# A graph network's first layer on one core: half of the type one-hots moved from VectorE to ScalarE, multiplied one chunk later

## The reference, cut to what matters

```python
def rel_layer(h, src, dst, etype, norm, V, comp, loop_w, bias, activation):
    c = comp[etype]                       # (100000, 8): a row of 8 coefficients by the edge's type
    m = 0
    for b in range(8):
        m = m + c[:, b, None] * (h @ V[b])[src]
    agg = segment_sum(m * norm, dst)
    out = agg + bias + h @ loop_w
    return relu(out) if activation else out

h = relu(layernorm(x))
x = x + rel_layer2(rel_layer1(h))         # both with the same etype, norm, src and dst
h = relu(layernorm(x))
x = x + gcn(relu(gcn(h)))                 # deg, the degree of a node, scales its rows
```

## Time and profile before

| | us |
|---|---|
| median of 3 runs (lowest, highest) | 2038.98 (2038.0, 2039.23) |
| the profiled execution | 2035.34 |
| its span, from the first to the last instruction | 2033.6 |
| busy in the span: TensorE, VectorE | 1691.0, 1404.2 |
| busy in the span: GpSimd, ScalarE | 1403.0, 356.8 |

### The profile page before, as it was taken

One profiled execution on the slowest core, in us unless ns is written; L12 is line 12 of the kernel. 1 busy time (PEld: TensorE's weight loads), 2 busy tenths in 40 slices (PEclk: granted clock), 3 DMA queues, 4 the chain that ended last, 5 costly groups with the idle time before them and its releaser, 6 DMA issues. The chain is left out here.

```text
span 2033.6 us, 40639 instructions
## 1 busy us (share of the span) xinstructions
PE 1691.0 (83%) x12305; PEld 1214.2 (60%) x12306; DVE 1404.2 (69%) x2294; ACT 356.8 (18%) x869; POOL 1403.0 (69%) x1527
## 2 busy tenths in 40 slices
PE   1488888788788888888389988889999899968998
PEld 1366556566566565566366666666676666745564
DVE  7898888888888878886677566566666657511533
ACT  2032222222222222222101111011011101100300
POOL 5777777777777777777477777777777777777000
PEclk8589889889899899898699888899999899978999
DMA  5334343343343333332222222233232332334473
GB/s 149 92 101 113 94 109 98 96 109 97 92 112 94 93 110 94 98 102 71 72 61 62 60 60 59 58 84 100 85 102 68 82 97 77 92 94 127 148 238 118
DMA packets 194039, 196.66 MB, mean 97 GB/s; under 512 B 109132, under 2 KB 157273, under 8 KB 193946
## 3 DMA queue, kind: packets, MB, share of 16 engines
q0 software_dynamic: 45760, 93.81, 16.8%
q1 hardware_dynamic: 140134, 97.59, 16.5%
q10 hardware_dynamic: 8052, 4.04, 0.7%
HBM read 169.75 MB, written 25.57 MB: 96 GB/s over the span
## 5 line engine op out<-in xcount | busy, mean ns | idle before, releaser
L811 POOL DMA_INDIRECT ring<-h_rows,rel_idx x1312 | 1257.7, 959 | 400.5 <-issue 365.4
L986 DVE TENSOR_TENSOR rel_pick<-rel_src_row,dve_bank 128x1664 bf16<-128x1664 int32 (+1 forms) x268 | 486.0, 1814 | 176.9 <-PE rel_ps_p L1215 93.4
L1284 PE MATMUL rel_ps_z<-rel_C,ring 128*128 128x56 f32 x3100 | 417.9, 284 | 166.6 <-DMA ring<-h_rows,rel_idx 83.2
L1284 PEld LDWEIGHTS rel_ps_z<-rel_C,ring 128*128 128x128 f32 x3100 | 399.4, 200 | 219.0 <-issue 209.8
L1382 ACT ACTIVATE rel_ZT<-rel_ps_z 128x304 f32 x292 | 114.2, 426 | 1071.3 <-PE rel_ps_z L1284 1069.7
L1228 PE MATMUL rel_ps_p<-rel_h_parts,rel_pick 128*128 128x384 bf16 x1150 | 266.8, 363 | 0.0
L1372 ACT ACTIVATE rel_A<-rel_ps_a 128x500 f32 x292 | 165.6, 603 | 391.3 <-PE rel_ps_a L1172 206.2
L1215 PE MATMUL rel_ps_p<-rel_h_parts,rel_pick 128*128 128x384 bf16 x1100 | 202.2, 345 | 22.0 <-DVE rel_h_parts L974 22.0
L1215 PE MATMUL carried<-rel_h_parts,rel_pick 128*128 128x384 bf16 x1100 | 190.7, 332 | 2.4 <-DVE rel_pick L986 2.4
L1172 PE MATMUL rel_ps_a<-rel_M,rel_lo 128*128 128x175 bf16 x784 | 156.8, 296 | 38.3 <-DVE rel_M L953 38.1
L1215 PEld LDWEIGHTS rel_ps_p<-rel_h_parts,rel_pick 128*128 128x128 bf16 x1100 | 113.4, 105 | 100.2 <-issue 39.5
(11 more groups left out here) (232 smaller groups left out, 1699.6 us busy)
## 6 DMA issues: line engine op xcount, KB each, us to landing
ring<-h_rows,rel_idx POOLq DMA_INDIRECT x1312
A_slabs<-rel_A SPq DMA_DIRECT2D x25, 800.0 KB
A_slot<-A_slabs SPq DMA_DIRECT2D x25, 800.0 KB, 4.5
rel_types<-edge_types SPq DMA_DIRECT2D x97, 200.0 KB
early_slot<-A_slabs SPq DMA_DIRECT2D x18, 896.0 KB, 6.1
rel_src_row<-in_src_dram SPq DMA_DIRECT2D x134, 64.0 KB, 3.0
last_slot<-A_slabs SPq DMA_DIRECT2D x4, 512.0 KB, 6.0
ring<-h_rows,idx_table POOLq DMA_INDIRECT x118
```

Source lines behind the costliest of these rows:

```text
L811: g_.indirect_dma_start(ring[:, s * CHUNK + i, :], None, rows_in, bass.IndirectOffsetOnAxis(ap=idx[which][:, n:n + 1], axis=0)).then_inc(l ...
L986: v.tensor_tensor(pick[:, b0:b0 + n, :], src_row[s][:, :].unsqueeze(1).to_broadcast(shape), node_ids[:, b0:b0 + n].unsqueeze(2).to_broadca ...
L1284: ins = m_.matmul(bank(ps_z[s], NB)[:, :, bass.ds(at[i], TW)], ring[:, first + i, :], C[s][:, i, :, :], start=False, stop=(i == n - 1))
```

## The change

The one-hot of types 0 to 99 stays on VectorE. That of types 100 to 199 is made on ScalarE in two passes over the types t: first (t - k)^2, k being the partition's type number (as a bias of -k, `less_type`), then relu(1 - that), which is 1 where t = k and 0 elsewhere (bias 1, `one_col`). ScalarE makes it after its two copies of A and before its copy of ZT. The type product stands one chunk later on TensorE: in chunk c that of c + 5, not of c + 6, while the one-hots are still made for c + 6. The sums follow one chunk later too (`scale` of c + 4, not c + 5). The degree product moves on TensorE from behind the type product to ahead of the picks of its chunk. The waits of GpSimd for type products are lowered by one where the product moved. `prepare` gets one memset and one small VectorE operation for the two bias tables.

```diff
@@ prepare @@
+            g.memset(t.one_col[:, :], 1.0).then_inc(consts_set, 1)
...
+            v.tensor_scalar(t.less_type[:, :], t.type_id[0:RH, :], -1.0, None, ALU.mult)
@@ new class @@
+class SharedCoefficients(Coefficients):
...
+    def load(self, eng, m, s):
+        after(eng, self.upper_ready, m - 1)
+        super().load(eng, m, s)
+
+    def make_onehot(self, eng, m, quarter_m, s):
+
+        after(eng, self.product_done, m - 1)
+        eng.wait_ge(self.etype_in[s], (quarter_m + 1) * 16)
+        self.nc.vector.tensor_scalar(self.onehot[:, s % 2, 0, :], self.etype[:, s % 2, :], self.t.type_id[0:RH, 0:1],
+                                     None, ALU.is_equal).then_inc(self.onehot_ready, 1)
+
+    def make_upper(self, act, m, quarter_m, s):
+
+        after(act, self.product_done, m - 1)
+        act.wait_ge(self.etype_in[s], (quarter_m + 1) * 16)
+        upper = self.onehot[:, s % 2, 1, :]
+        self.nc.scalar.activation(upper, self.etype[:, s % 2, :], ACT.Square, bias=self.t.less_type[:, 1:2]).then_inc(self.squared, 1)
+        act.wait_ge(self.squared, m + 1)
+        self.nc.scalar.activation(upper, upper, ACT.Relu, bias=self.t.one_col[:, 0:1], scale=-1.0).then_inc(self.upper_ready, 1)
+
+    def multiply(self, eng, m, s):
+        eng.wait_ge(self.upper_ready, m + 1)
+        super().multiply(eng, m, s)
@@ GpSimd, half_way and ahead_of @@
-                    hold(pool, co.product_done, at + (AHEAD + 1) if not (isinstance(c, int) and at + (AHEAD + 1) > ET_CHUNKS) else ET_CHUNKS)
+                    hold(pool, co.product_done, at + AHEAD if not (isinstance(c, int) and at + AHEAD > ET_CHUNKS) else ET_CHUNKS)
...
-                    begun = {(5, 0): 1, (5, 1): 3, (6, 0): 5, (6, 1): 6, (7, 0): 7, (7, 1): 8}
+                    begun = {(5, 0): 1, (5, 1): 3, (6, 0): 4, (6, 1): 5, (7, 0): 6, (7, 1): 7}
@@ VectorE @@
                     co.make_onehot(dve, m, m // 4, m % 4)
-                    if m:
-                        co.scale(dve, m - 1, m - 1)
+                    if m >= 2:
+                        co.scale(dve, m - 2, m - 2)
...
-                    if layer == 0 and not (isinstance(c, int) and c + AHEAD - 1 >= ET_CHUNKS):
-                        co.scale(dve, c + (AHEAD - 1), (parity * CPG + j + AHEAD - 1) % COEF_RING)
+                    if layer == 0 and not (isinstance(c, int) and c + AHEAD - 2 >= ET_CHUNKS):
+                        co.scale(dve, c + (AHEAD - 2), (parity * CPG + j + AHEAD - 2) % COEF_RING)
@@ TensorE @@
-                for m in range(AHEAD):
+                for m in range(AHEAD - 1):
                     co.multiply(pe, m, m % 2)
...
                         sum_slab(c, j % 2, at)
+                    if layer == 0 and j == 3 and not is_first:
+                        degrees(g - 1)
...
-                    if makes(g, j):
-                        co.multiply(pe, c + AHEAD, j % 2)
+                    if layer == 0 and not (isinstance(c, int) and c + AHEAD - 1 >= ET_CHUNKS):
+                        co.multiply(pe, c + (AHEAD - 1), (j + 1) % 2)
...
-                    if layer == 0 and j == 3 and not is_first:
-                        degrees(g - 1)
@@ ScalarE @@
+            for m in range(AHEAD if layer == 0 else 0):
+                co.make_upper(act, m, m // 4, m % 4)
...
                         spread_slab(g, j, parity, at[4:6], 1)
...
+                    if makes(g, j):
+                        co.make_upper(act, c + AHEAD, g + (j + AHEAD) // 4, (j + AHEAD) % 4)
                     spread(g, j, parity, at, s)
```

More of the change, by code:

```diff
@@ L340, in _ @@
             k.link(v.tensor_reduce(t_min[:, :], dst_f[:, :, :], AX.X, ALU.min))
-            dve.wait_ge(consts_set, 19)
+            dve.wait_ge(consts_set, 20)
             cols = [P, RAW, P]
@@ L496, in scale, with __init__ @@
         ins.then_inc(self.coef_ready, 1)
+class SharedCoefficients(Coefficients):
+    def __init__(self, nc, io, t, ctx, name):
+        super().__init__(nc, io, t, ctx, name)
+        self.squared, self.upper_ready = semaphore(nc, t, ctx, f"{name}_squared"), semaphore(nc, t, ctx, f"{name}_upper_ready")
+    def load(self, eng, m, s):
[16 more added lines that the diff above has]
+        super().multiply(eng, m, s)
 class Finish:
@@ L687, in relational_layer @@
             deg_sum, deg_summed, deg_chain = sb("deg_sum", [P, P], F32), sem("deg_summed"), sem("deg_chain")
-            co = Coefficients(nc, io, t, ctx, name)
+            co = SharedCoefficients(nc, io, t, ctx, name)
             sources, ps_p = 2, [ps("ps_p")]
@@ L1987, in program @@
         t.comp = sb("comp_parts", [RH, 2, 3, 2 * NB], BF16)
+        t.less_type, t.one_col = sb("less_type", [RH, 2], F32), sb("one_col", [RH, 1], F32)
         t.group_lo = sb("group_lo", [P, GROUPS], F32)
```

## The result

The changed kernel takes 2062.65 us (median of 4 runs, 2058.81 to 2066.23) where the kernel before takes 2038.49 us (4 runs, 2035.43 to 2039.23): a ratio of 1.0116, 95% interval 1.0102 to 1.0129. It is 24 us slower. The forecast was 2035.1 us with a range up to 2043, so it was wrong, and on the side to which it gave the least chance.

A forecast was written before the change was run, and what follows sets the result against it. GpSimd's gathers were taken to bound layer 0. Gathers -5.5, start +1.5 and +0.1, compute and tail nothing: 2035.34 became 2031.4 for the profiled execution, and the median 2038.98 - 3.9 = 2035.1 us, range 2029 to 2043.

The forecast's parts named there:

- What bounds the kernel before: Layer 0: GpSimd's 736 gathers set its end; VectorE and TensorE are faster, some 0.25 us per chunk.
- GpSimd's gathers: Layer 0: VectorE's halved one-hot time lengthens gathers less, -5.5 us, between bounds of 0 and 11.0 us.
- Folds stay as they are: Layer 0 gathers: the lengthening by VectorE's folds was taken as unchanged.
- The literal rule of the Trainium skill: VectorE's two-port instructions block GpSimd until their end; the change would free up to 42 us; chance 1 in 100.
- The start: First chunks of layer 0: chunk 3 ends about 5.2 us late, GpSimd stalls 1.2 to 2 us: +1.5 us, and +0.1.
- The pace of compute: Layer 0's middle: costs nothing while four chunks take VectorE and TensorE under 38.2 us; now about 37.4.
- Sum per group: VectorE and TensorE over four chunks: added and removed waits give -1.2 us, about 36.2 us per group.
- The rival with a chance of 0.13: Chunks j = 1 and 2: VectorE's new wait for the product makes compute the bound; 2 us beyond is +30, 2069.
- The price of being over: Layer 0: each us per group beyond 38.2 costs 24 us over 24 groups, less 15 us of lead.
- the tail: End of layer 0, behind chunk 96's rows: same order as before, 0, with 2 us to each side.
- The degree product ahead: j = 3: VectorE no longer waits 2.50 us for the degree product behind the type product; 2.1 us gained.

The follow-up runs named there:

- the last two rows above: The changed kernel with both repairs, ratio 0.9974, and that kernel with both one-hot halves on VectorE, 2038.32 us, ratio 1.0011.
- both repairs: The changed kernel with SyncE's slab store ahead of the type load and VectorE's one-hot just ahead of the sums: 2033.34 us, ratio 0.9974.

## Why the prediction was wrong, point by point

**What bounds the kernel before: right.** The degree product alone freed 3.3 us of compute per group and the time stayed (ratio 1.0014).

**GpSimd's gathers: right for the one-hots, wrong for the folds.** Forecast -5.5 us. Where ScalarE's half is all that differs and GpSimd is the bound (the last two rows above), the share of the one-hots falls by 6.2 us; from the kernel before to the changed one it falls by 4.6. But "Folds stay as they are" failed: their share goes from 2.7 to 9.3 us with nothing changed in them but where they meet the gathers. Of the 14 ns that a gather of the changed kernel lost, about half is this (4.7 us of folds, 4.6 of one-hots), and no merit of the forecast. With both repairs the folds go the other way and cost 1.8 us more than without ScalarE's half, so that only 6 ns per gather are left. In the kernel with the store first, the stretch from the first gather of chunk 8 (119.8) to that of chunk 96 (959.4) is 839.6 us against 845.1 before, 5.5 less. The literal rule of the Trainium skill ("SBUF — State Buffer", section "SBUF: two separate sides", an exclusive lock for a whole instruction) would, by the prediction's estimate, have made the gain up to 42 us; no run came near that.

**The start: half right, and under-sized.** Walked: the chunk 3 end of TensorE near 116.9; measured 117.50, where the earlier trace rows has 111.66. ScalarE's passes, for which there was no row, take 1,139 and 1,148 ns on average where I had 1.13 us. The Trainium skill ("ScalarE: Activation LUTs", section "What ACT_TABLE_LOAD costs") gives 280 ns + 0.833 ns per element with one pointer operand, 1,133 ns for 1,024 elements, and the trace agrees. But the stall was to be 1 to 2 us and is 5.53, chunk 8 3.6 us late for a forecast of 1.6. Two slips: GpSimd came to its wait at 113.0 and not at 115.7 (the 115.57 of the earlier trace rows is the start of a gather; its last gather ahead of it ended at 115.1 then and at 113.0 now), and between the start of TensorE's last row and the gather lie another 1.7 us (117.50 to 119.20), which I left out. Nor was ScalarE the main cause of the stall: without its half chunk 8 is still 3.1 us late (118.7), and with VectorE's one-hot behind, it is not late at all (114.9). It is VectorE's wait for the product in the first chunks. The one-hot ahead of chunk 0 begins at 73.09, 3.1 us late where I had walked 4.2, and then the lateness of TensorE's chunk ends grows from 2.8 us in chunk 0 to 3.5, 4.1 and 5.8 in chunk 3, where I had walked 0.3 to 0.5 per chunk.

**The pace of compute: the step that failed.** The prediction says "Sum per group: +1.3 - 0.4 - 2.1 = -1.2, about 36.2 us. So compute is faster". It walked VectorE's and TensorE's queues and not SyncE's. The type load that now waits for ScalarE was costed at the start of the layer and not in the layer's middle, where the slab store stands behind it. With the store moved ahead, the pace is 35.9 us, the walked number to 0.3 us; with the store behind, 38.6. A fold that waits 44.6 / 21 = 2.1 us in a group moves the pace by 2.7. Its lateness may run on to TensorE and back to ScalarE's half, on which the next load waits; that circle is argued from the rows of one group, and no run took it apart. That 36.2 and 35.9 agree so well bears out the sum of the walk, not each of its three terms, which no run prices singly.

It takes two waits. The four combinations of the late store and VectorE's early one-hot wait are all measured:

| | one-hot ahead (waits for the product) | one-hot behind |
|---|---|---|
| slab store behind the load | 38.6 us per group, 2062.65 us | 37.3, 2029.53 us |
| slab store first | 35.9, 2036.22 us | 33.7, 2033.34 us |

Each wait costs compute 1.3 to 3.6 us per group, but only the corner in which both stand lies over GpSimd's pace (38.0 to 38.4), and only that corner is slow. The rival with a chance of 0.13 had the right kind (VectorE's new wait makes compute the bound), and the run with the later product alone shows that its mechanism exists (2072.67 us). With the degree product ahead, as the change has it, that wait is not enough: 2042.66 us without ScalarE's half. All three slow kernels have it, each time with a partner: the late store, the degree product behind, or both.

**The price of being over: wrong in form.** The rival was to cost 24 us per us beyond 38.2, "less 15 us of lead". By that, 0.4 us beyond costs nothing; it cost 24 us. The lag of compute behind GpSimd is no credit but a debt: before, it melted from 26 us at chunk 12 to 3 at chunk 96, and at the barrier only the 3 were left. In the changed kernel 23 are left there, and they fall due in the tail, which I had put at nothing. So the cost does not begin where compute's pace passes GpSimd's, but where the lag no longer melts in time, and the kernel before stands just at that point: no fast kernel has a lag over 4.2 us at chunk 96, and none of the slow ones one under 23. An estimate from the paces between chunks 12 and 84 (37.5 before, 38.6 in the change, 39.1 with the later product only, 40.9 in the change with the degree product behind): each us over 37.5, times the 21 groups from chunk 12 to chunk 96, makes 23, 34 and 71 us; measured 24.2, 35.0 and 67.5. No run has such a pace between 37.6 and 38.6, so the beginning of that line is worked out and not seen. In the slowest kernel the last gather of the layer begins 49.8 us later than before (1026.65 for 976.87), and the gap behind it is 21.5 us longer. The gap between those two gathers shows the debt directly: 39.8 to 41.8 us in the three slow kernels, 19.3 to 23.6 in all the others. This is the slowest kernel's first gather behind the barrier, 41.81 us after its last one, and then that of the kernel with the store first, 23.14 us:

```profile
1069.40 0.94 POOL L869 DMA_INDIRECT ring<-h_rows,idx_table  x1 [41.81 <-POOLq L696]
```
```profile
999.66 0.94 POOL L869 DMA_INDIRECT ring<-h_rows,idx_table  x1 [23.14 <-POOLq L696]
```

**The degree product ahead: right in sign.** 3.3 us per group in the kernel before, 1.0 with the later product (38.6 to 37.6; 1.5 between chunks 12 and 84), 2.1 in the changed kernel (40.7 to 38.6). In the kernel before that is worth nothing to the time; in the changed one, with compute as the bound, over 40 us.

**What stays open.** The kernel with one-hots behind and the late store has gathers of 956 ns, with both repairs 964; their ratios' intervals overlap between 0.9963 and 0.9971. The table of the gathers says where most of the 8 ns lies, in the folds (4.8 us and 9.3, with 2.4 beside one-hots in both), but not what sets where a fold meets a gather, and no run tests that. How the store's lateness grows from 2.1 to 2.7 us per group was not taken apart either.

## What to carry to other kernels

When an edit puts a wait in front of a queue's entry, walk every entry that stands behind it on that queue, all through the loop: here a DMA that needed nothing of the new wait was held by it, and moving one store ahead of one load gave 26 us back. When one engine bounds a stretch and another lags behind it, write down the lag and the pace at which it melts: what is left of it at the next barrier is paid there, so a slower pace can cost time before it passes the first engine's. And test each suspected wait with the other one in place and with it gone, since two that are harmless alone can cross the bound together.

## What the runs showed of the hardware

A gather of 0.94 us on GpSimd is lengthened where VectorE's one-hots or folds run beside it. In the kernel before, 96 gathers beside one-hots are 8.6 us longer in all, 40 beside folds 7.4, and 478 beside neither 2.0. The amount goes with where the two meet and not only with how much VectorE does: the same folds cost the gathers 2.7 us in one kernel and 9.3 in another, and the mean gather is 970 ns with 0.88 us of one-hots per chunk, and 956 to 964 with half of that. ScalarE's two passes per chunk over 1,024 elements (1.14 and 1.15 us) beside those gathers made them no longer: 970 ns without the passes, 964 with them.
